# Masking the diagonal of attention on GpSimd, weighting later, and an early start for the last down projection

## The chip, the cores and the metric

One core of a Trainium2 chip. The metric is device time in microseconds (us), the median of several runs. The core's engines are TensorE (PE in the profile; its weight loads are PEld), VectorE (DVE), ScalarE (ACT), GpSimd (POOL) and SyncE (SP, which only starts transfers here).

## The reference, cut to what matters

Two transformer layers on x of shape (2, 512, 512), fp32 throughout, each with a modulation by c. Layer 0 has causal attention and a mixture of low-rank experts; layer 1 has a linear "attention" block, a gated feed-forward with low-rank additions, and a last gated feed-forward whose weights are 4-bit codes with scales.

```python
# layer 0, attention: 32 heads, 8 key/value groups of 4 heads, head width 16
scores = einsum('bihd,bjhd->bhij', q, k) * HD ** -0.5
scores = where(tril(ones((s, s))), scores, finfo.min)
out = einsum('bhij,bjhd->bihd', softmax(scores), v).reshape(b, s, -1) @ wo
...
# layer 1, twice (with low-rank terms the first time, without the second)
h = silu(x @ Wg.T) * (x @ Wu.T)        # 512 -> 1792
x = x + gb * (h @ Wd.T)                # 1792 -> 512
```

## The kernel before, in words

Every engine has one program written out by hand, and semaphores join them; there is no planner. TensorE's results are numbered jobs (`job_list`, line 114). Job j goes into PSUM bank j % 8, and `begin` (line 1373) waits until the job eight places earlier has been freed. Every fp32 product is made of three reduced-precision ones (lines 1383 to 1385): high by high, low by high, high by low, so each operand is rounded on ScalarE ("round") and its remainder subtracted on VectorE ("split").

*Attention* (lines 1472 to 1531 on TensorE). The work is 64 units: 2 batches by 8 groups by 4 query tiles of 128 rows. Unit n has ic = n % 4 and looks at ic + 1 key blocks, so units of a group are one, two, three and four blocks long. Step n of TensorE's loop has up to three parts:
- `scores(n)` (1477): for each of 4 heads a matmul (1485) and a bf16 matmul (1487) that adds -1e30 above the diagonal. Only the row maxima are taken from these. The two halves (heads 0, 1 and heads 2, 3) wait for the maxima of unit n-1, and VectorE's `reduce_max` (1178) makes two maxima per unit.
- `transposed(n - 2)` (1491): the scores again, key by query, one matmul per block (1500) with the maxima subtracted through extra rows of QS. GpSimd writes these rows (659) as the product of the identity and the maxima, two instructions per unit. For the diagonal block a bf16 matmul (1503) adds the mask. ScalarE takes the exponential of each block (798) into one of 10 tiles PT. Three PSUM banks (4 to 6) take the blocks in turn.
- `weighted` (1508): for two units at once, in even steps, for units n-4 and n-3. Values by exponentials, 32-row tiles (1517), into bank 7 for a whole group.

When a group is complete, its numerators and denominators leave bank 7: for even groups on ScalarE (`copy_even`, 504, called at unit 4 of eight), for odd ones on VectorE (`copy_odd`, 1096, at unit 2 of the next eight). VectorE then handles the pair: `swap_sums` at unit 3, `invert` in two halves at 4 and 5, `divide` at 6. ScalarE rounds the divided heads (`round_heads`, at the units in `ROUND_AT`, line 80) and VectorE splits them (`split_heads`, `SPLIT_AT`). Decoding of the 4-bit weights of layer 1 rides along: curves on ScalarE (758), their sums on VectorE (1066, at units 0, 1 and 7 of eight), scaling and adding in halves on GpSimd (615, 629).

After the loop VectorE splits the output weights WO (1199), which ScalarE rounds near the end (810), the remaining heads, the last pair's copy, swap, reciprocals and division (1200 to 1209), while TensorE multiplies the output projection `wo`; GpSimd subtracts weights (676) and adds the results to x (643).

*Layer 1, feed-forward, n = 0 and 1* (lines 1628 to 1699). `gu`: 14 pieces of gate and up, 48 or more matmuls each. For n = 0 a thin product `td` follows (1656). Then `gates` (1430), two small products that spread the gate row over the partitions, which VectorE copies into GAB (1038). Then `down`: eight banks for the eight row tiles; for n = 0 first x1 is added by identity matmuls (1666); then for each of 14 hidden tiles k and each row tile three matmuls (1680 to 1682). The hidden tile k is rounded into HH[k % 4] (912) and split into HL[k % 4] (1094). HH and HL also hold the input of gate up, so `round_hidden` of the first four waits for gate up's last matmul (906). At the end of `gu`, VectorE's order is: two hidden splits, weight piece split and scaling, for n = 1 then the gate copies (1343), then the rest. TensorE asks for all eight banks before the first matmul of `down` (1660).

## Time and profile before

| | us |
|---|---|
| median of 3 runs | 995.11 |
| lowest, highest | 993.63, 998.77 |
| the profiled execution | 996.45 |
| its span | 994.7 |
| TensorE busy, of the span | 913.2 (92%) |
| VectorE | 684.5 (69%) |
| ScalarE | 528.1 (53%) |
| GpSimd | 190.6 (19%) |
| the attention loop | about 88 to 292 |
| last gate up ends, last down starts | 900.1, 907.6 |

A matmul's busy time includes its way through the pipeline, so the distance between starts says more than its length. In a row of the timeline the columns are start, length, engine, line, operation, output and inputs, count, and in brackets the idle time before it with what ended it. In a row of groups the columns are line, engine, operation, names and shapes, count, busy us and mean ns of one, and the idle time before them with its releasers.

### The profile page before, as it was taken

Reading aid. Unit: us, or ns where it says so; the run is one execution under the profiler, and the core shown is the slowest. Engines: PE = TensorE matmul, PEld = TensorE weight load, DVE = VectorE, ACT = ScalarE, POOL = GpSimd, SP = SyncE. Lnnn points to the kernel's source line nnn. Section 1 sums busy time; section 2 is a strip of 40 time slices with the busy share of each in tenths; the row PEclk is TensorE's granted clock in tenths of the full one; section 3 lists DMA queues with packets and bytes.
Section 4 is the critical chain, followed back from the end, with each engine's and each line's share of the span. In section 5 each row is a group of like instructions: output and inputs, shape, how many; then the busy total and the mean of one; then the engine's idle time right before and its main releaser. Section 6 shows DMA issues by size and latency. Waiting matters only on the chain.

```text
span 994.7 us, 13863 instructions
## 1 busy us (share of the span) xinstructions
PE 913.2 (92%) x5316; PEld 702.4 (71%) x5316; DVE 684.5 (69%) x853; ACT 528.1 (53%) x683; POOL 190.6 (19%) x197
## 2 busy tenths in 40 slices
PE   3798899989899799999999999999969999997996
PEld 1565565555557587788888888688858888885885
DVE  4735788889989687777555554367887675666742
ACT  1503656666663335577555554267718666655730
POOL 3002546566666024100000000000040000000003
PEclk9798999999999899999999999789989999998999
DMA  9387466566422022016332332023302333332102
GB/s 330 125 240 148 60 109 105 67 107 107 81 86 96 11 64 74 22 40 192 96 95 87 95 88 71 1 85 106 106 22 77 95 104 106 86 105 64 43 1 84
DMA packets 40161, 91.60 MB, mean 92 GB/s; under 512 B 6944, under 2 KB 10144, under 8 KB 40096
## 3 DMA queue, kind: packets, MB, share of 16 engines
q1 hardware_dynamic: 35824, 85.23, 34.0%
q10 hardware_dynamic: 4272, 5.49, 1.6%
q8 instruction: 42, 0.69, 0.3%
q14 instruction: 23, 0.19, 0.1%
HBM read 76.02 MB, written 2.10 MB: 79 GB/s over the span
## 4 chain that ended last, share of the span: by engine, by line
PE 68%; DVE 6%; issue 3%; ACT 1%; POOL 1%; POOLq 0%; DVEq 0%; ACTq 0%
PE PS L1383 14%; PE PS L1385 14%; PE PS L1384 14%; PE PS L1680 5%; PE PS L1681 5%; PE PS L1682 5%; PE PS L1485 1%; PE PS L1517 1%; PE PS L1666 1%; PE PS L1616 1%; PE PS L1615 1%; POOL X L643 1%; DVE MX L1178 1%; PE PS L1500 1%; PE PS L1423 1%
## 5 line engine op out<-in xcount | busy, mean ns | idle before, releaser
L758 ACT ACTIVATE PL<-CODE 128x1024 f32<-128x1024 int32 x200 | 201.5, 1055 | 45.4 <-DVE ACC L1066 41.4
L1383 PE MATMUL PS<-HH,WRH 128*128 128x512 f32 x448 | 174.8, 390 | 0.0
L1384 PE MATMUL PS<-HH,WRL 128*128 128x512 f32 x448 | 174.5, 390 | 0.0
L1385 PE MATMUL PS<-HL,WRH 128*128 128x512 f32 x448 | 174.5, 390 | 0.0
L643 POOL TENSOR_TENSOR X<-X,SCR 128x512 f32<-128x512 f32 x32 | 42.2, 1328 | 601.4 <-DVE SCR L1051 601.3
L1066 DVE SCALAR_TENSOR_TENSOR ACC<-PL,ACC 128x1024 f32<-128x1024 f32 x100 | 124.5, 1245 | 8.4
L798 ACT ACTIVATE PT<-PS 128x512 f32<-128x512 f32 x160 | 85.2, 604 | 66.7 <-PE PS L1500 47.9
L1331 DVE TENSOR_TENSOR HID<-SG,PS 128x512 f32<-128x512 f32 x56 | 38.3, 685 | 114.2 <-PE PS L1616 68.4
L1178 DVE TENSOR_REDUCE MX<-PS 128x2 f32<-128x256 f32 (+3 forms) x128 | 99.5, 818 | 18.6 <-PE PS L1487 11.2
L659 POOL TENSOR_TENSOR QS<-ident,MX 64x256 fp32r<-64x256 f32 x128 | 97.1, 759 | 66.2 <-DVE MX L1178 59.2
L1485 PE MATMUL PS<-KS,QS 128*128 128x128 f32 (+3 forms) x256 | 84.0, 410 | 15.9 <-DVE MX L1178 14.4
L1383 PEld LDWEIGHTS PS<-HH,WRH 128*128 128x128 f32 x448 | 84.4, 188 | 17.6
L1384 PEld LDWEIGHTS PS<-HH,WRL 128*128 128x128 f32 x448 | 84.4, 188 | 17.6
L1385 PEld LDWEIGHTS PS<-HL,WRH 128*128 128x128 f32 x448 | 84.2, 188 | 17.4
L1680 PE MATMUL PS<-WRH,HH 128*128 128x512 f32 x224 | 89.3, 399 | 5.4 <-DVE GAB L1038 5.4
L1681 PE MATMUL PS<-WRL,HH 128*128 128x512 f32 x224 | 89.0, 397 | 0.0
L1682 PE MATMUL PS<-WRH,HL 128*128 128x512 f32 x224 | 88.8, 397 | 0.0
L1066 DVE SCALAR_TENSOR_TENSOR ACC<-PL 128x1024 f32<-128x1024 f32 x50 | 62.1, 1243 | 14.2 <-ACT PL L758 14.0
L930 ACT ACTIVATE SG<-PS 128x512 f32<-128x512 f32 x56 | 32.7, 589 | 73.3 <-PE PS L1616 46.1
L1485 PEld LDWEIGHTS PS<-KS,QS 128*128 128x128 f32 x256 | 51.1, 201 | 28.9 <-issue 13.8
L767 ACT ACTIVATE ACC<-ACC 128x1024 f32<-128x1024 f32 x50 | 53.1, 1062 | 31.1 <-DVE ACC L1066 31.1
L1500 PE MATMUL PS<-QS,KN 128*128 128x512 f32 x160 | 58.1, 443 | 7.4 <-ACT PT L798 7.0
(222 smaller groups left out, 1590.1 us busy)
## 6 DMA issues: line engine op xcount, KB each, us to landing
CODE<-in_CODES SPq DMA_DIRECT2D x50, 512.0 KB, 3.5
SCALE<-in_SCALES SPq DMA_DIRECT2D x100, 256.0 KB, 4.2
WM<-in_WM SPq DMA_DIRECT2D x12, 1024.0 KB, 7.2
QS<-FH SPq DMA_DIRECT2D x32, 128.0 KB, 4.1
QS<-FL SPq DMA_DIRECT2D x32, 128.0 KB, 5.2
X<-in_X ACTq DMA_DIRECT2D x2, 1024.0 KB, 12.4
out_x<-X ACTq DMA_DIRECT2D x8, 256.0 KB, 2.0
WF<-in_LBGU SPq DMA_DIRECT2D x14, 128.0 KB, 2.0
```

Source lines behind the costliest of these rows:

```text
L659: nc.gpsimd.tensor_tensor(QS[64:P, q % STACKS, :, ic * P + 64 * half:ic * P + 64 * half + 64], ident[rows, rows].unsqueeze(1).to_broadcast ...
L758: nc.scalar.activation(PL[:, n % 3], CODE[:, p % 2], ACT.Prelu, scale=scale, bias=bias, alpha=alpha).then_inc(s_plane, 1)
L798: nc.scalar.activation(block_of(n, jc)[:].rearrange("p h i -> p (h i)"), PS[:, 4 + done % 3], ACT.Exp, scale=HD ** -0.5).then_inc(s_exp, 1)
L1066: nc.vector.scalar_tensor_tensor(acc, PL[:, at_plane % 3], CAPS[i], rest_of, ALU.min, ALU.add).then_inc(s_used, 1)
L1178: nc.vector.reduce_max(MX[:, n % 2, 2 * pair:2 * pair + 2], PS[:, 2 * pair:2 * pair + 2, 0:w], AX_X).then_inc(s_mx, 1)
L1383: nc.tensor.matmul(dst, lh, rh, start=start and k == 0, stop=False)
L1384: nc.tensor.matmul(dst, ll, rh, start=False, stop=False)
L1385: ins = nc.tensor.matmul(dst, lh, rl, start=False, stop=stop and k == KC - 1)
L1485: nc.tensor.matmul(PS[:, h, 0:(ic + 1) * P], QS[:, q % STACKS, h, ic * P:(ic + 1) * P], KS[:, q % STACKS, 0:(ic + 1) * P], start=True, sto ...
L1680: nc.tensor.matmul(dst[t], hh, wh, start=(n == 1 and k == 0), stop=False, skip_group_check=True)
L1681: nc.tensor.matmul(dst[t], hh, wl, start=False, stop=False, skip_group_check=True)
L1682: ins = nc.tensor.matmul(dst[t], hl, wh, start=False, stop=last and n == 1, skip_group_check=True)
```

## The change

Four parts. (1) The bf16 mask matmul on the transposed diagonal block goes. GpSimd instead runs an `affine_select` over the diagonal block of exponentials in PT (128 x 512, zero where the key is behind the query), one per unit, before it waits for the maxima of the unit three later; TensorE's weighting waits for it. (2) Weighting moves from even steps (units n-4, n-3) to odd ones (n-5, n-4). `copy_even` and `copy_odd` come two units later, and so do swap and reciprocals; the division goes to unit 0 of the next eight. The last but one pair's division, rounding and split move behind the loop. (3) The gates of the last down projection are made after the last norm instead of after gate up. Its first hidden tile gets buffers of its own (HF, LF0), and is rounded and split after piece 7 of gate up. (4) Both down projections ask for each bank at its first use.

```diff
-ROUND_AT = {41: 0, 46: 1, 49: 2, 54: 3, 58: 4, 60: 5, 62: 6}
+ROUND_AT = {41: 0, 46: 1, 49: 2, 54: 3, 59: 4, 61: 5}
...
+            def cut(n):
+
+                block = block_of(n, n % TB)
+                pool.wait_ge(s_exp, STC(n // TB) + (n % TB + 1) * (n % TB + 2) // 2)
+                nc.gpsimd.affine_select(block[:], block[:], [[0, REP], [1, P]], ALU.is_ge, 0.0, base=0,
+                                        channel_multiplier=-1).then_inc(s_tri, 1)
+                pool.wait_ge(s_tri, n + 1)
+
             for n in range(B * GROUPS * TB):
                 q, ic = divmod(n, TB)
+                if n >= 3:
+                    cut(n - 3)
                 pool.wait_ge(s_mx, 2 * n + 2)
...
+            for n in range(B * GROUPS * TB - 3, B * GROUPS * TB):
+                cut(n)
             for half in range(2):
                 scale_half(N_QKV - 1, half)
...
-                if n % 8 == 4:
+                if n % 8 == 6:
                     copy_even(act, n // TB - 1)
...
+            round_heads(B - 1, PAIRS - 2)
             act.wait_ge(s_pv, units)
...
             def round_hidden(n, k):
-                i = HS_N[n] + k
-                if k < 4:
+                if (n, k) == (1, 0):
+                    act.wait_ge(s_mm, J["down", 0, NT - 1] + 1)
+                elif k < 4:
                     act.wait_ge(s_mm, J["gu", n, MC - 1, B - 1, 1] + 1)
...
+                    if (n, m) == (1, MC // 2):
+                        round_hidden(1, 0)
...
-                for k in range(2):
+                for k in range(n, 2):
                     round_hidden(n, k)
...
-                if pair_at(n, 2) is not None:
-                    copy_odd(pair_at(n, 2))
-                if pair_at(n, 3) is not None:
-                    swap_sums(pair_at(n, 3))
+                if pair_at(n, 4) is not None:
+                    copy_odd(pair_at(n, 4))
+                if pair_at(n, 5) is not None:
+                    swap_sums(pair_at(n, 5))
                 for half in range(2):
-                    if pair_at(n, 4 + half) is not None:
+                    if pair_at(n, 5 + half) is not None:
                         invert(half)
-                if pair_at(n, 6) is not None:
-                    divide(pair_at(n, 6))
+                if n >= 16 and n % 8 == 0:
+                    divide(n // 8 - 2)
...
-            for pair in range(PAIRS, last):
+            for pair in range(PAIRS, last - 1):
                 split_heads(pair)
+            divide(last - 1)
             copy_odd(last)
             gates("ga0")
             swap_sums(last)
+            split_heads(last - 1)
...
+                    if (n, m) == (1, MC // 2):
+                        hidden_split(1, 0)
...
-                if n == 1:
-                    gates(f"g{n}")
...
                 if n == 0:
                     modulate(3, B - 1)
+                    gates("g1")
...
-                                           QS[:, q % STACKS, :, ic * P:(ic + 1) * P], start=True, stop=jc < ic)
-                    if jc == ic:
-                        ins = nc.tensor.matmul(dst, maskB[:], identB[:].unsqueeze(1).to_broadcast([P, REP, P]),
-                                               start=False, stop=True)
+                                           QS[:, q % STACKS, :, ic * P:(ic + 1) * P], start=True, stop=True)
...
-                    pe.wait_ge(s_exp, blocks[1])
+                    if jc < ic:
+                        pe.wait_ge(s_exp, blocks[1])
+                    else:
+                        pe.wait_ge(s_tri, n + 1)
...
-            for n in range(units + 3):
+            for n in range(units + 4):
...
-                if n >= 3 and n % 2 == 0:
-                    for unit in (n - 4, n - 3):
+                if n >= 5 and n % 2 == 1:
+                    for unit in (n - 5, n - 4):
                         weighted(unit)
...
-                gates(f"g{n}", 1, n)
-                dst = [begin(("down", n, t)) for t in range(NT)]
+                if n == 0:
+                    gates("g0", 1, 0)
+                dst = [PS[:, bank(("down", n, t))] for t in range(NT)]
...
+                        if (n, k) == (1, 0):
+                            begin(("down", n, t))
...
                 if n == 0:
                     for b in range(B):
                         norm(3, b)
+                    gates("g1", 1, 1)
```

In the order of jobs the two gates of n = 1 move likewise, behind the last norm.

## Rows read from the trace of the kernel before

**Rows 1.** Table by stage: stretch, its length, PE, PEld, DVE, ACT, POOL busy, PEclk, DMA share, GB/s.

```profile
92.00:292.00 200.00, 179.79 (x2002) 116.62 (x2002) 170.22 (x201) 125.16 (x212) 116.03 (x143) 0.99 0.55 89
...
800.00:900.00 100.00, 100.00 (x443) 82.67 (x441) 62.79 (x61) 61.19 (x71) 0.00 (x0) 1.00 0.32 95
...
908.00:912.00 4.00, 4.00 (x11) 3.03 (x11) 3.90 (x4) 2.15 (x3) 0.00 (x0) 0.50 0.36 87
```

**Rows 2.** Groups on VectorE from 92 to 292 us; the last one over the whole run.

```profile
L1178 DVE TENSOR_REDUCE MX<-PS 128x2 f32<-128x1024 f32 x32 | 37.7, 1219 | 8.1 <-issue 4.4 <-PE PS L1487 3.1 <-DVE NUM L1119 0.4
L1178 DVE TENSOR_REDUCE MX<-PS 128x2 f32<-128x768 f32 x32 | 29.2, 953 | 6.0 <-PE PS L1487 4.1 <-POOL QS L659 1.5
L1114 DVE RECIPROCAL DENS<-DENS 128x256 f32<-128x256 f32 x14 | 24.4, 1743 | 0.0
L1178 DVE TENSOR_REDUCE MX<-PS 128x2 f32<-128x512 f32 x30 | 19.3, 683 | 3.3 <-PE PS L1487 3.0
L1066 DVE SCALAR_TENSOR_TENSOR ACC<-PL,ACC 128x1024 f32<-128x1024 f32 x12 | 16.3, 1358 | 0.0
L1178 DVE TENSOR_REDUCE MX<-PS 128x2 f32<-128x256 f32 x30 | 11.4, 417 | 0.5 <-PE PS L1487 0.3
...
L1102 DVE SCALAR_TENSOR_TENSOR NUM<-PS,HALVES,NUM 128x512 f32<-128x512 f32 x7 | 5.3, 751 | 7.0 <-PE PS L1517 7.0
...
L1119 DVE TENSOR_TENSOR NUM<-NUM,DENS 128x512 f32<-128x512 f32 x7 | 4.8, 681 | 0.0
...
L1066 DVE SCALAR_TENSOR_TENSOR ACC<-PL,ACC 128x1024 f32<-128x1024 f32 x100 | 124.5, 1245 | 8.4
```

**Rows 3.** Timeline of TensorE in attention, from 200.13 to 225.33 us.

```profile
200.13 0.38 PE L1485 MATMUL PS<-KS,QS 128*128 128x256 f32 x1
...
203.01 0.52 PE L1485 MATMUL PS<-KS,QS 128*128 128x384 f32 x1
...
204.32 0.48 PE L1500 MATMUL PS<-QS,KN 128*128 128x512 f32 x1
204.64 0.39 PE L1503 MATMUL PS<-identB,maskB 128*128 128x512 bf16 x1
204.96 1.74 PE L1517 MATMUL PS<-PT,V 128*32 128x128 f32 x56
206.62 0.50 PE L1485 MATMUL PS<-KS,QS 128*128 128x512 f32 x1
...
208.08 0.71 PE L1500 MATMUL PS<-QS,KN 128*128 128x512 f32 x2
...
225.33 0.38 PE L1485 MATMUL PS<-KS,QS 128*128 128x256 f32 x1
```

**Rows 4.** The chain of waits from 240 to 270 us, shares of the 30 us.

```profile
by line: DVE MX L1178 19.9%; issue 16.5%; PE PS L1485 12.0%; DVE DENS L1114 11.1%; PE PS L1517 11.1%; ACT PT L798 7.3%; PE PS L1500 4.6%; PE PS L1487 3.5%; ACT PL L758 3.1%; PE PS L1503 3.1%; DVE DENS L1110 2.5%; DVE NUM L1119 2.0%; DVE DEN
```

**Rows 5.** Timeline of TensorE at the start of the last down projection.

```profile
900.18 1.98 PE L1435 MATMUL PS<-MR,sel 2*128 2x512 f32 x4
907.56 0.76 PE L1680 MATMUL PS<-WRH,HH 128*128 128x512 f32 x1 [5.40 <-DVE GAB L1038]
```

**Rows 6.** Groups on GpSimd: the diagonal products from 92 to 292 us, the others over the run.

```profile
L659 POOL TENSOR_TENSOR QS<-ident,MX 64x256 fp32r<-64x256 f32 x126 | 95.1, 754 | 63.4 <-DVE MX L1178 56.5
...
L643 POOL TENSOR_TENSOR X<-X,SCR 128x512 f32<-128x512 f32 x32 | 42.2, 1328 | 601.4 <-DVE SCR L1051 601.3
...
L607 POOL MEMSET KN<- 64x512 f32 x2 | 1.0, 520 | 44.9 <-PE PS L1452 44.8
```

**Rows 7.** The even copies on ScalarE, from 92 to 292 us.

```profile
L509 ACT ACTIVATE NUM<-PS,HALVES 128x512 f32<-128x512 f32 x8 | 5.5, 688 | 8.3 <-PE PS L1517 8.3
```

**Rows 8.** Timeline behind the attention loop: the last division on VectorE, a subtraction on GpSimd.

```profile
297.74 4.61 POOL L676 TENSOR_TENSOR ATL<-ATF,ATH 128x2048 fp32r<-128x2048 f32 x1
...
300.82 2.08 DVE L1119 TENSOR_TENSOR NUM<-NUM,DENS 128x512 f32<-128x512 f32 x1
```

**Rows 9.** Timeline of TensorE at the start of the first down projection.

```profile
634.93 0.30 PE L1666 MATMUL PS<-identR,HH 128*128 128x128 f32 x1 [0.88 <-DVE GAB L1038]
```

More of the change, by code:

```diff
@@ L179, in job_list @@
                 jobs.append((("td", b), 1))
-        gates(f"g{n}")
+        if n == 0:
+            gates("g0")
         for t in range(NT):
@@ L319, in build @@
         LDBL = sb("LDBL", [P, D], F32R, R0 + 96 * K)
+        HF = sb("HF", [P, T], F32R, R0 + 86 * K)
+        LF0 = sb("LF0", [P, T], F32R, R0 + 94 * K)
         SCR = sb("SCR", [P, 2, D], F32, R0 + 100 * K)
@@ L363, in build @@
         s_exp = sem("exponentials_ready")
+        s_tri = sem("diagonal_blocks_cut")
         s_pv = sem("values_weighted")
@@ L525, in hidden_used, with hidden_parts @@
                 eng.wait_ge(s_mm, J["down", n, NT - 1] + 1)
+        def hidden_parts(n, k):
+            return (HF[:], LF0[:]) if (n, k) == (1, 0) else (HH[:, k % 4], HL[:, k % 4])
         def tile_transposed(eng, u):
@@ L1093, in hidden_split @@
                 dve.wait_ge(s_hsh, HS_N[n] + k + 1)
-                nc.vector.tensor_tensor(HL[:, k % 4], HID[:, k], HH[:, k % 4], ALU.subtract).then_inc(s_hsl, 1)
+                high, low = hidden_parts(n, k)
+                nc.vector.tensor_tensor(low, HID[:, k], high, ALU.subtract).then_inc(s_hsl, 1)
             def copy_odd(pair):
@@ L1338, in _ @@
                         rest(TDL[:, cols], ("td", b), TDH[:, cols])
-                    gates(f"g{n}")
-                for k in range(2):
+                    gates("g0")
+                for k in range(n, 2):
                     hidden_split(n, k)
                 finish(p)
-                if n == 1:
-                    gates(f"g{n}")
                 for i in range(MC // 2):
@@ L1368, in _ @@
                     modulate(3, B - 1)
+                    gates("g1")
         @block.tensor
@@ L1676, in _ @@
                         cols = slice(t * P, (t + 1) * P)
-                        hh, hl = HH[:, k % 4, cols], HL[:, k % 4, cols]
+                        high, low = hidden_parts(n, k)
+                        hh, hl = high[:, cols], low[:, cols]
+                        if (n, k) == (1, 0):
+                            begin(("down", n, t))
                         wh, wl = WRH[:, slot(p), w], WRL[:, slot(p), w]
```

4 lines of the change are left out of this document (3 added, 1 removed).

## The prediction

> **What bounds the kernel now.** I read the page first (its chain of work that ended last is TensorE for 68% of the span), then a table by stage, then the two stages that the diff touches. Two kinds of stage appear. In the projections TensorE never stops, and only its own gaps are worth anything. In attention (92 to 292 us) no engine fills the time: of 200 us VectorE is busy 170.2, GpSimd 116.0, ScalarE 125.2 [rows 1]; TensorE's 179.8 overlaps its own pipeline and says less. That stage is a relay. Scores of unit n+1 wait, half by half, for the row maxima of unit n, and VectorE's next maxima wait for those scores, so roughly each unit costs the longer of what TensorE and what VectorE do in it.
>
> VectorE's share of a unit is two maxima, 0.84, 1.36, 1.9 or 2.44 us for the four lengths, plus whatever rides on that unit: reciprocals of 1.74, curve sums of 1.36, a division of 0.68, copies of 1.5 for numerator and denominator with a wait of 1.0 before them [rows 2]. TensorE's share is read from one stretch of its timeline [rows 3]: scores take 1.3 us for the third unit of a group (203.01 to 204.32) and 1.46 for the fourth, a transposed block 0.28 to 0.32, weighting two long units 1.66 (204.96 to 206.62). The chain passes through both engines [rows 4].
>
> The second place is the start of the last down projection. Gate up ends at 900.1, four gate matmuls start, and then TensorE idles 5.40 us for the gate copies, which VectorE makes only after two hidden splits and two weight pieces; its next full matmul is at 907.56 and TensorE's granted clock is 0.50, its 1.2 GHz level, from 908 to 912 [rows 1, 5].
>
> **The change part by part.**
>
> *Mask on the scores goes from TensorE.* 64 bf16 matmuls leave. The next instruction starts 0.32 us behind one (204.64 to 204.96) [rows 3]; 64 of them are at most 20 us of TensorE's time, and nothing where TensorE waits anyway. The row maxima keep their own mask matmuls. Only what is on the chain counts: in the 30 us of [rows 4] L1503 has 3.1%, 0.93 us, four masks of about nine.
>
> *Mask goes to GpSimd.* 64 selections over 128x512 in fp32, each waiting for the exponential and then for itself. None is in the trace. Below it lies a fill of 64x512, no input, 0.52 us; above, a 128x512 operation of two inputs, 1.33 us [rows 6]. One input lies between; the middle is 0.92, rounded to 0.90, which I take, keeping both ends. GpSimd then has 116.0 + 64 x 0.90 = 174 us, and with about 0.07 us between dependent instructions (some 210 of them; two diagonal products of 0.61 come as 1.30 in the timeline) 189 us. That fits under 200, with little spare. Behind the selection on its queue stand the diagonal products of unit n, which TensorE needs two steps later, and VectorE's next but one maxima; a unit of slack hides the selection as long as GpSimd's sum stays under the stage. The row of diagonal products shows that slack: GpSimd sat idle 56.5 us there for maxima [rows 6].
>
> The Trainium skill (GPSIMD Engine Reference, section 3.1) gives 1.8 cycles an element at best for a one-input style loop, 769 ns for 512 elements; by that figure GpSimd would stand at 180 us instead of 189 and the sum would not change. No row here shows it.
>
> *Weighting one step later, copies and divisions two units later.* Waits leave: VectorE stood 7.0 us before seven odd copies, ScalarE 8.3 us before eight even ones, because the weighting was issued in the same step as the copy [rows 2, 7]. Now it is a step old when the copy asks. But the load is dealt out anew. TensorE's step n is scores (0.6, 1.0, 1.3, 1.46 by the length), the transposed blocks of unit n-2 (3, 4, 1, 2 of 0.3), a mask of 0.25, and in every second step a weighting (1.66 for a long pair, 24/56 of it, 0.7, for a short one). Eight units, step by step:
> - before, TensorE 2.5, 2.5, 3.5, 2.3 twice; VectorE 2.2, 2.7, 3.4, 3.2, 2.6, 3.1, 2.6, 3.8. The larger of each pair, summed: 24.9. The trace has 25.2, from 200.13 to 225.33 [rows 3].
> - after, TensorE 1.5, 2.9, 1.6, 3.7 twice (weighting now shares a step with the long fourth unit); VectorE 2.9, 2.7, 1.9, 2.4, 2.3, 3.8, 3.6, 3.8, since swap, reciprocals and division stand at the sixth unit, the seventh and the next first. The larger of each pair: 25.0.
>
> So pair by pair nothing is won: TensorE's relief falls where VectorE was already the longer. What is won comes from slack between neighbours. VectorE's own sum is 22.5 in eight units (13.1 of maxima, 2.25 curve sums, 6.4 for the pair of groups) and cannot shrink; its idle time is 2.7. Afterwards I find one real hole, at the fourth unit (TensorE 3.7 + 0.6 for the next scores, VectorE 2.4: 1.5 us when it has no arrears and the hand-offs are taken in), and small ones of 0.4 together. Idle 1.9 instead of 2.7, eight times: **-6 us**. The bounds are VectorE's sum (-21) and no gain at all (0).
>
> Against that stands contention. A division that takes 0.68 us elsewhere took 2.08 for the last pair, and ended at 302.90, half a microsecond after GpSimd's 4.61 us subtraction that ran from 297.74 [rows 8]. Some 30 VectorE instructions of two inputs in memory lie in the stage; curve sums average 1.36 us there [rows 2] against 1.25 for one that nothing disturbs (the mean of all 100 of the run, most of them with GpSimd idle), a loss of 0.11 with GpSimd 58% busy. At some 95% busy that is 0.18: 30 x 0.07 = **+2 us**. If each of the 30 lost half a selection, as that division lost more, it would be 30 x 0.45 = +13, and the kernel would end at 995 us. The Trainium skill (SBUF - State Buffer, "Who interferes with whom") has such an exclusion, for the whole instruction, of a VectorE instruction with two SBUF inputs and a GpSimd instruction that reads SBUF. By that rule the trace agrees in kind; its average of 0.11 is smaller.
>
> *End of attention.* The weighting of units 60 and 61 (0.8 us) moves behind the last transposed block; the even copy (1.4) now stands before the rounding of the output weights in place of a head's rounding (0.65), and VectorE already waits 3.6 us for that rounding; one division (0.7) moves into VectorE's tail. The last selection is covered by 2.3 us of weighting. Masks saved, 0.5. **+1 us** (0 to 3).
>
> *First down projection.* Its banks are asked for one by one, so the additions of x1 start when the gate matmuls are through, and not after the copies, for which TensorE idled 0.88 us before 634.93 [rows 9]: **-1 us**.
>
> *Second down projection.* The gates are made before gate up, and the first hidden tile is rounded and split into its own buffers in the middle of it (about 1.0 us of ScalarE and 1.2 of VectorE; both are busy some 62 of 100 us in gate up while TensorE is busy all of them [rows 1], so free). At its end TensorE goes straight on: the first tile's 24 matmuls last 5.4 us, in which the second is rounded (1.0) and split (1.2), and the last bank is wanted after 4.8 us. From 900.1 to 907.56 are 7.5 us; 11 matmuls at the 1.2 GHz level [rows 1], starting 0.43 us apart against 0.226 in gate up (443 in 100 us), cost 0.2 us too much each, 2.2. What returns is the gates' four matmuls, 1.7 us, now in front of gate up where TensorE is the bound. 7.5 + 2.2 - 1.7 = **-8 us**. If the clock falls anyway it is -6.
>
> **Sum.** -6 + 2 + 1 - 1 - 8 = -12. The profiled execution took 996.45 us (span 994.7), 1.3 above the median of 995.11; 996.45 - 12 = 984.45. I say **984 us**; by the median it would be 983.
>
> **The rivals.**
> 1. *Attention gains nothing.* The larger of each pair decides, or two-input instructions lose to GpSimd what the holes give: 0 in the stage, 0 + 1 - 1 - 8, so 988 us (995 with the full 13 on top of -6). For it: the pair sum above and the division of 2.08. Against: VectorE visibly catches up between units. 0.17, and 0.03 for the 995.
> 2. *GpSimd becomes the pace, and the kernel slower.* Its stage is 116.0 + 15 of hand-offs + 64c. From c = 1.08 us it passes 200; from about 1.2 it eats the other gains. At the two-input price of 1.33 (with the blocking that the row holds, [rows 6]) it is 216, +16 in place of -4: 16 + 1 - 1 - 8 = +8, so 1004 us. For it: the price is unknown and the engine's spare time small; TensorE would then wait for diagonal products. Against: one input, not two. 0.14 for slower, and 0.12 for a price of 1.1 to 1.25, where the time stays within 5 us of before.
> 3. *The last down projection doesn't start early:* ScalarE's rounding of the second tile, queued behind the last gate up, comes late. 1.0 + 1.2 us against 5.4 say no; then only the other terms stay, -4, so 992 us. 0.04.
>
> **How the numbers follow.** Forecast 0.5; rivals 0.2, 0.26 in two parts, 0.04. Range 971 to 1001: below, the attention bound of -21 with no contention gives 967, of which I take all but the last 4 us; above, rival 2 nearly to its price. Faster by over 0.5% (5 us, about what can be told from no change): 0.5 + 0.17 + 0.01 of rival 3 = 0.68; within: 0.12 + 0.03 + 0.03 = 0.18; slower: 0.14.
>
> **What would show it.** L1503 gone; 64 selections of 0.6 to 1.1 us, GpSimd busy near 175 us in the stage; copies with no wait for weighting; the stage 3 to 5 us shorter; VectorE busy still 170; waits of TensorE for diagonal products near 0. In the last down projection no idle before its first matmul and full clock through it. Wrong if the selections take over 1.1 us, or if waits for QS by L659 appear on TensorE or VectorE.

## The result: 1012.84 us, slower

Changed kernel: 1012.84 us, median of 4 runs (1011.61 to 1014.15). The kernel before beside it: 996.94 us (993.63 to 1003.13). Ratio 1.0152, 95% interval 1.0098 to 1.0207. I had said 984 us, 971 to 1001. The profiled execution took 1011.61 us, its span is 1009.9 (before 994.7), so the trace has 15.2 us to explain.

Three marks split the span: the start of the last pair of row maxima on VectorE (A), the start of the first transpose of LQF, the weight tile that TensorE turns behind the output projection (B), and the end. A is read from these rows, before and after:

```profile
282.64 2.36 DVE L1178 TENSOR_REDUCE MX<-PS 128x2 f32<-128x1024 f32 x2 [0.44 <-DVE NUM L1119]
```
```profile
303.49 2.36 DVE L1204 TENSOR_REDUCE MX<-PS 128x2 f32<-128x1024 f32 x2
```

| | A | A to B | B to end |
|---|---|---|---|
| before | 282.6 | 34.2 | 677.9 |
| after | 303.5 | 39.3 | 667.1 |
| difference | +20.9 | +5.1 | -10.8 |

So the stretch with the down projections is shorter by about what was forecast, and attention took back more than twice that. The profile after, first the page's busy times and TensorE's granted clock in tenths by fortieths of the span:

```profile
PE 912.9 (90%) x5252; PEld 704.8 (70%) x5252; DVE 691.2 (68%) x853; ACT 527.4 (52%) x683; POOL 229.5 (23%) x261
...
PEclk9798799998999989999999999979997999999999
```

The table by stage (columns as in [rows 1]):

```profile
92.00:292.00 200.00, 163.97 (x1683) 108.31 (x1686) 157.52 (x184) 109.91 (x187) 140.73 (x188) 0.92 0.53 82
800.00:900.00 100.00, 100.00 (x443) 82.84 (x443) 68.28 (x67) 64.82 (x75) 0.00 (x0) 1.00 0.33 97
```

VectorE, my bound of the stage, is busy 157.5 of 200 us instead of 170.2: it waits more. And the clock is new: 0.92 where [rows 1] has 0.99. The groups that answer to [rows 2, 6, 7], from VectorE (92 to 292), GpSimd (whole run) and ScalarE (92 to 292):

```profile
L1204 DVE TENSOR_REDUCE MX<-PS 128x2 f32<-128x768 f32 x30 | 27.8, 954 | 15.8 <-PE PS L1516 15.7
...
L1204 DVE TENSOR_REDUCE MX<-PS 128x2 f32<-128x512 f32 x30 | 19.4, 686 | 8.8 <-POOL QS L678 6.6 <-PE PS L1516 1.9
L1091 DVE SCALAR_TENSOR_TENSOR ACC<-PL,ACC 128x1024 f32<-128x1024 f32 x12 | 16.3, 1362 | 0.0
...
L1145 DVE TENSOR_TENSOR NUM<-NUM,DENS 128x512 f32<-128x512 f32 x6 | 6.7, 1117 | 0.0
...
L1128 DVE SCALAR_TENSOR_TENSOR NUM<-PS,HALVES,NUM 128x512 f32<-128x512 f32 x6 | 4.5, 742 | 0.0
```
```profile
L678 POOL TENSOR_TENSOR QS<-ident,MX 64x256 fp32r<-64x256 f32 x128 | 88.0, 687 | 41.4 <-DVE MX L1204 33.0
L666 POOL TENSOR_SCALAR_AFFINE_SELECT PT<-PT 128x512 f32<-128x512 f32 x64 | 48.0, 750 | 8.6 <-ACT PT L819 4.0
```
```profile
L514 ACT ACTIVATE NUM<-PS,HALVES 128x512 f32<-128x512 f32 x7 | 4.9, 702 | 0.0
```

The selection costs 0.75 us (0.90 forecast), and the copies' waits for weighting are gone as forecast (0.0 where 7.0 and 8.3 stood). What took their place is in the waits from 88 to 312 us (the engine and line that waits, what it waits for, then us in all, how often, and the longest):

```profile
ACT PT L819 <- PE PS L1529: 96.3, 52, 3.6
...
PE PS L1529 <- ACT PT L819: 18.1, 14, 3.0
...
DVE MX L1204 <- POOL QS L678: 13.6, 9, 2.2
...
PE PS L1529 <- POOL QS L678: 10.4, 9, 1.6
```

Before, the last two kinds were 1.5 us [rows 2] and 0.3, and TensorE's wait for ScalarE's exponentials was 7.0. So TensorE waits for ScalarE to empty a PSUM bank, and TensorE and VectorE wait for GpSimd's diagonal products. TensorE's wait for ScalarE comes about once per eight units, here unit 8k+6 with the even copy, a curve pair, then the four exponentials of unit 8k+7:

```profile
222.29 1.58 ACT L819 ACTIVATE PT<-PS 128x512 f32<-128x512 f32 x3 [2.63 <-PE PS L1529]
...
223.74 0.70 ACT L514 ACTIVATE NUM<-PS,HALVES 128x512 f32<-128x512 f32 x1
...
224.31 0.71 ACT L514 ACTIVATE DEN<-PS,HALVES 128x512 f32<-128x512 f32 x1
...
224.88 2.03 ACT L779 ACTIVATE PL<-CODE 128x1024 f32<-128x1024 int32 x2
...
226.77 2.08 ACT L819 ACTIVATE PT<-PS 128x512 f32<-128x512 f32 x4
...
227.44 0.50 PE L1529 MATMUL PS<-QS,KN 128*128 128x512 f32 x1 [2.71 <-ACT PT L819]
```

TensorE stands 2.71 us. Before, its longest gap between 100 and 280 us was 1.03 us and its clock 1.00 throughout; now it has twelve gaps over 1.1 us there, and over the 20 us from 220 the clock is 0.91.

### The profile page after: what moved, and what is told of

Read it like the earlier page. It is cut to its first block, busy times and chain, and to the rows that moved or that the text cites. A ratio compares the mean times of both kernels' runs of the same rounds, so it can differ in the third digit from the quotient of the medians.

```text
span 1009.9 us, 13854 instructions
## 1 busy us (share of the span) xinstructions
PE 912.9 (90%) x5252; PEld 704.8 (70%) x5252; DVE 691.2 (68%) x853; ACT 527.4 (52%) x683; POOL 229.5 (23%) x261
## 4 chain that ended last, share of the span: by engine, by line
PE 73%; DVE 10%; POOL 5%; issue 5%; ACT 4%; DMA 1%; POOLq 0%; SPq 0%; DVEq 0%; ACTq 0%
PE PS L1412 15%; PE PS L1413 14%; PE PS L1414 14%; PE PS L1715 5%; PE PS L1716 5%; PE PS L1717 5%; PE PS L1514 3%; DVE MX L1204 3%; POOL QS L678 2%; ACT PT L819 2%; PE PS L1546 2%; PE PS L1529 1%; DVE DENS L1140 1%; DMA WM<-in_WM 1%; PE PS L1645 1%
## 5 line engine op out<-in xcount | busy, mean ns | idle before, releaser
L1204 DVE TENSOR_REDUCE MX<-PS 128x2 f32<-128x256 f32 (+3 forms) x128 | 100.4, 820 | 39.3 <-PE PS L1516 24.9
L1514 PE MATMUL PS<-KS,QS 128*128 128x128 f32 (+3 forms) x256 | 89.2, 427 | 14.3 <-DVE MX L1204 12.0
L678 POOL TENSOR_TENSOR QS<-ident,MX 64x256 fp32r<-64x256 f32 x128 | 88.0, 687 | 41.4 <-DVE MX L1204 33.0
L1529 PE MATMUL PS<-QS,KN 128*128 128x512 f32 x160 | 60.6, 462 | 28.8 <-ACT PT L819 18.1
L1715 PE MATMUL PS<-WRH,HH 128*128 128x512 f32 x216 | 85.0, 393 | 0.0
L1716 PE MATMUL PS<-WRL,HH 128*128 128x512 f32 x216 | 84.9, 393 | 0.0
L1717 PE MATMUL PS<-WRH,HL 128*128 128x512 f32 x216 | 84.7, 392 | 0.0
L1514 PEld LDWEIGHTS PS<-KS,QS 128*128 128x128 f32 x256 | 55.2, 218 | 31.0 <-DVE MX L1204 18.7
```

What stands on the lines that cost most here:

```text
L678: nc.gpsimd.tensor_tensor(QS[64:P, q % STACKS, :, ic * P + 64 * half:ic * P + 64 * half + 64], ident[rows, rows].unsqueeze(1).to_broadcast ...
L1204: nc.vector.reduce_max(MX[:, n % 2, 2 * pair:2 * pair + 2], PS[:, 2 * pair:2 * pair + 2, 0:w], AX_X).then_inc(s_mx, 1)
L1514: nc.tensor.matmul(PS[:, h, 0:(ic + 1) * P], QS[:, q % STACKS, h, ic * P:(ic + 1) * P], KS[:, q % STACKS, 0:(ic + 1) * P], start=True, sto ...
L1715: nc.tensor.matmul(dst[t], hh, wh, start=(n == 1 and k == 0), stop=False, skip_group_check=True)
L1716: nc.tensor.matmul(dst[t], hh, wl, start=False, stop=False, skip_group_check=True)
L1717: ins = nc.tensor.matmul(dst[t], hl, wh, start=False, stop=last and n == 1, skip_group_check=True)
```

## The experiments

Theories at the start. **Q**: the selections stand ahead of the diagonal products on GpSimd's queue and wait there for ScalarE. **L**: GpSimd's sum of work. **S**: the new schedule costs by itself, because the even copy and curves now stand before the exponentials of the long fourth unit. Later texts call S in its narrower forms C (ScalarE's burst of copy and curves leaves TensorE without a free bank), "clock" (the gaps then lower TensorE's clock) and W (the later weighting itself is what costs), and L "pace". All results, with marks A and B and the clock over 92 to 292 us from each profiled execution:

| kernel | median, us | ratio, 95% | clock | A | A to B | B to end |
|---|---|---|---|---|---|---|
| e1 down alone | 989.3 | 0.987 to 0.995 | 0.99 | 282.9 | 34.1 | 667.2 |
| e2 mask on TensorE | 1011.8 | 1.009 to 1.019 | 0.92 | 299.9 | 38.0 | 674.7 |
| e3 selection alone | 1030.2 | 1.030 to 1.036 | 0.89 | 317.5 | 33.0 | 678.1 |
| e4 cut behind | 1022.3 | 1.020 to 1.030 | 0.91 | 310.3 | 37.7 | 672.1 |
| e5 curves behind | 1002.7 | 0.999 to 1.007 | 0.96 | 295.8 | 37.3 | 670.1 |
| e6 e2, gap filled | 1000.5 | 1.000 to 1.005 | 0.99 | 290.2 | 34.1 | 673.5 |
| e7 weighting even | 1027.3 | 1.025 to 1.034 | 0.88 | 322.7 | 33.5 | 669.0 |
| e8 e5 with cut | 1013.1 | 1.011 to 1.022 | 0.89 | 306.3 | 37.7 | 673.5 |
| e9 after, filled | 1010.0 | 1.009 to 1.016 | 0.96 | 297.0 | 40.4 | 670.5 |
| e10 curves ahead | 1002.2 | 1.000 to 1.008 | 0.96 | 290.4 | 38.0 | 674.7 |
| e11 e9, scale later | 996.6 | 0.997 to 1.002 | 0.96 | 289.1 | 40.2 | 670.4 |
| e12 e11, ATL later | 993.1 | 0.990 to 0.998 | 0.99 | 284.9 | 34.2 | 672.1 |
| e13 mended | 992.2 | 0.992 to 0.996 | 0.95 | 285.2 | 36.3 | 668.7 |
| e14 burst planted | 1014.8 | 1.011 to 1.019 | 0.95 | 299.3 | 36.7 | 668.8 |
| e15 e13, filled | 992.0 | 0.990 to 0.996 | 0.96 | 284.4 | 34.2 | 672.1 |
| e16 e14, filled | 1002.9 | 1.004 to 1.008 | 0.97 | 298.1 | 34.7 | 671.2 |

The medians of the kernel before in these sessions were 996.1 to 999.0.

**The change taken apart: e1 to e3.** e1 is the kernel before with the edits of the two down projections only. e2 is the changed kernel with the mask matmul put back and no selection. e3 is the kernel before with the selection only:

```diff
 # e2, from the changed kernel
-                if n >= 3:
-                    cut(n - 3)
...
-                                           QS[:, q % STACKS, :, ic * P:(ic + 1) * P], start=True, stop=True)
+                                           QS[:, q % STACKS, :, ic * P:(ic + 1) * P], start=True, stop=jc < ic)
+                    if jc == ic:
+                        ins = nc.tensor.matmul(dst, maskB[:], identB[:].unsqueeze(1).to_broadcast([P, REP, P]),
+                                               start=False, stop=True)
...
-                    if jc < ic:
-                        pe.wait_ge(s_exp, blocks[1])
-                    else:
-                        pe.wait_ge(s_tri, n + 1)
+                    pe.wait_ge(s_exp, blocks[1])
```

> Only the two down projections are changed (parts 3 and 4): early gates, own buffers for the first hidden tile, banks asked for one by one. All theories of the attention stage expect the same: the attention loop as before (last row maximum near 285 us) and about 9 us less in all, a ratio near 0.991. If instead the time is as before, the gain of the last down projection is given back somewhere behind it.

> The changed kernel with the selections taken out and the mask matmul back on TensorE; weighting, copies and divisions stay late. Theory Q (GpSimd's queue: the selection stands before the diagonal products and waits for ScalarE) and theory L (GpSimd's sum of work) expect the attention stage at or under its time of before, the kernel at 985 to 990 us. Theory S (the new schedule itself costs: even copy and curves stand before the exponentials of the long fourth unit) expects the stage to stay some 15 us longer, the kernel near 1010 us.

> The kernel before with the selection alone (mask matmul off TensorE, selection on GpSimd before the maxima wait); weighting in even steps, copies and down projections as before. Theory S expects it at or under the time before, 985 to 997 us. Theories Q and L expect it slower by 10 us or more, 1005 to 1025 us, since TensorE now even has one step less between exponential and weighting.

e1 gives 8 us and is the fastest of the three kernels so far. e2 is as slow as the whole change: without one selection the schedule alone moves A from 282.9 to 299.9. That is theory S; Q and L, which expected 985 to 990 us, do not explain the bulk of the loss. For e3 it is the other way round: S expected 985 to 997 us, Q and L a loss, and the selection costs 33 us, since the weighting in even steps asks for its result at once. The waits of e3, 88 to 312 us:

```profile
PEld PS L1530 <- POOL PT L658: 32.7, 19, 2.9
PE PS L1530 <- POOL PT L658: 29.1, 20, 2.4
```

TensorE waits there for the selected block itself, which neither Q nor L had. The later weighting is thus what makes room for the selection; together they come out near where the schedule alone does (3.6 us behind it at A).

**Where the selection stands: e4** puts `cut(n - 3)` behind the diagonal products of unit n.

```diff
-                if n >= 3:
-                    cut(n - 3)
                 pool.wait_ge(s_mx, 2 * n + 2)
...
                     pool.wait_ge(s_dg, 2 * n + half + 1)
+                if n >= 3:
+                    cut(n - 3)
```

> The changed kernel with each selection moved behind the two diagonal products of its step on GpSimd's queue instead of before them. The work on every engine is the same. Theory Q expects most of the loss back, 985 to 995 us, and waits for QS near 0. Theory L expects no more than 3 us of difference from the changed kernel (1010 us), theory S none.

Worse by 9.5 us: the weighting now waits for the selection (PE L1546 on PT L666, below). Q was half right: the waits for QS fell as it said, from 10.4 to 1.2 us on TensorE and from 13.6 to 1.0 on VectorE, but the time that it expected back did not come, since the selection is late for the weighting instead. L and S, which expected little or no difference, didn't have that wait either.

```profile
PEld PS L1546 <- POOL PT L666: 17.1, 14, 2.0
...
PE PS L1546 <- POOL PT L666: 13.4, 13, 1.8
```

**What in the schedule costs: e5, e6, e7, e10**, all on e2. e5 runs the curves of unit 8k+6 behind unit 8k+7, e10 ahead of the copy, behind 8k+5. e6 leaves everything in place and issues one product of TensorE seven times, in front of the gap (each time afresh, so the result is the same). e7 puts the weighting back into even steps.

```diff
 # e5
                     copy_even(act, n // TB - 1)
-                ride(n + 3)
+                else:
+                    if n % 8 == 7:
+                        ride(n + 2)
+                    ride(n + 3)
 # e10
                     copy_even(act, n // TB - 1)
-                ride(n + 3)
+                else:
+                    ride(n + 3)
+                if n % 8 == 5:
+                    ride(n + 4)
 # e6
-                    ins = nc.tensor.matmul(dst, KN[q % STACKS][:, jc * P:(jc + 1) * P],
+                    for x in range(7 if n % 8 == 7 and jc == 2 else 1):
+                        ins = nc.tensor.matmul(dst, KN[q % STACKS][:, jc * P:(jc + 1) * P],
```

> The kernel with the new schedule and the mask still on TensorE (e2_mask_on_tensore, 1011.8 us), with one edit: on ScalarE the curves that followed the even groups' copy (behind unit 8k+6) run behind the exponentials of unit 8k+7. Theory C (ScalarE's burst of copy and curves ahead of the long fourth unit leaves TensorE without a free bank, and the gap then halves TensorE's clock for some microseconds): the gaps of 1.3 to 2.9 us ahead of the fourth unit's last transposed block shrink below 1 us, the granted clock over 92 to 292 us goes from 0.92 back above 0.96, and the time comes to 995 to 1002 us. Theory W (weighting two units at a time at odd steps, one unit later, is itself what costs): 1008 to 1014 us, clock unchanged.

> e2_mask_on_tensore with the gap filled and nothing moved: in every unit 8k+7 the third transposed block's product is issued seven times instead of once (each time afresh, the last one counts), which is work for about 1.3 to 1.5 us in the place where TensorE otherwise waits for ScalarE. Theory C with the clock as the larger part: the granted clock over 92 to 292 us rises above 0.96 although six useless products per eight units are added, and the time falls to 998 to 1006 us. If the wait itself is the cost and the clock only goes with it: 1010 to 1014 us or, where the products are not hidden, up to 1020 us.

> e2_mask_on_tensore with the weighting put back to the even steps; copies, swaps and divisions stay two units later. Theory W: 988 to 995 us, since the later weighting is the costly part. Theory C: ScalarE's copy and curves still stand ahead of the fourth unit, so the gaps and the clock of 0.92 stay and the time is 1006 to 1014 us.

> e2_mask_on_tensore with the curves that followed the even groups' copy moved ahead of it, behind unit 8k+5 (e5 moved them behind unit 8k+7, which made VectorE wait up to 4.2 us for their planes and so left gaps before the scores). Theory clock: neither gap is left, clock over 92 to 292 us 0.98 or more, 992 to 999 us. If the later weighting costs by itself even without gaps, as e6's 1000.5 us with useless products allows: 999 to 1004 us with the clock at 0.98 or more.

e6 is the telling one: 48 useless products on the busiest engine make the kernel 11 us faster, and A comes 9.7 us earlier. Nothing else was moved. The stage in e2, then in e6:

```profile
92.00:292.00 200.00, 177.24 (x1802) 113.82 (x1802) 159.29 (x189) 111.94 (x190) 105.58 (x134) 0.92 0.54 83
```
```profile
92.00:292.00 200.00, 186.35 (x1954) 122.60 (x1955) 167.66 (x198) 116.56 (x200) 110.98 (x140) 0.99 0.53 82
```

Only A speaks for the clock of the stage. Another 3.9 us of the gain in these two profiled executions lie between A and B: there a split on VectorE took 4.67 us in e2, since it started behind a long GpSimd subtraction, and 0.87 in e6, where it started before it, and the clock was 0.91 in e2 and 1.00 in e6. TensorE's wait is hardly longer in sum in e2 than in e1: its two groups with idle time, of e1 and then of e2, 92 to 292 us, hold 21.8 and 23.8 us of it.

```profile
L1498 PE MATMUL PS<-KS,QS 128*128 128x384 f32 (+3 forms) x248 | 81.9, 412 | 14.5 <-DVE MX L1190 14.5
L1513 PE MATMUL PS<-QS,KN 128*128 128x512 f32 x160 | 58.1, 443 | 7.3 <-ACT PT L806 7.0 <-POOL QS L667 0.3
```
```profile
L1510 PE MATMUL PS<-KS,QS 128*128 128x384 f32 (+3 forms) x239 | 85.4, 437 | 6.5 <-DVE MX L1200 6.2
...
L1525 PE MATMUL PS<-QS,KN 128*128 128x512 f32 x146 | 54.6, 455 | 17.3 <-ACT PT L815 15.9 <-POOL QS L676 1.1
```

It had become lumpy. TensorE's timeline in e2, behind one such gap:

```profile
224.90 0.80 PE L1525 MATMUL PS<-QS,KN 128*128 128x512 f32 x1 [2.71 <-ACT PT L815]
...
228.09 0.67 PE L1510 MATMUL PS<-KS,QS 128*128 128x384 f32 x1
...
228.66 0.67 PE L1510 MATMUL PS<-KS,QS 128*128 128x384 f32 x1
...
231.79 0.47 PE L1510 MATMUL PS<-KS,QS 128*128 128x512 f32 x1
...
232.14 0.47 PE L1510 MATMUL PS<-KS,QS 128*128 128x512 f32 x1
```

At 228 a score matmul of 384 columns with its mask comes every 0.57 us; at 231.8 one of 512 columns, a longer one, every 0.35. From 224.7 to 231.5 the granted clock is 0.50, TensorE's 1.2 GHz level. Between 100 and 290 us it is so four times, for 23.8 us together, each time behind a gap of 1.8 to 2.9 us. The Trainium skill (TensorE: Matmul & The Clock Gate, "HAM oscillation — how this bites in real kernels") describes matmul groups that each start at half rate because TensorE idled ahead of them; the trace agrees in kind. e5 and e10 made that gap shorter without useless work and gained 9 us each, somewhat less than expected: e5 made VectorE wait up to 4.2 us for the planes (what the curves leave for its sums), e10 keeps gaps of 1.1 to 1.7 us and a clock of 0.96, not the 0.98 of its forecast. In e7 the weighting of the next group asks for bank 7 before the late copy has emptied it; late copies need the late weighting:

```profile
PEld PS L1542 <- ACT DEN L514: 17.1, 7, 2.5
...
PE PS L1542 <- ACT DEN L514: 14.5, 7, 2.2
```

So C's forecast for e7 missed by 13 us, and e7 doesn't test W, since it brings a wait of its own. What speaks against W as the main cause is that e5, e6 and e10 leave the late weighting where it is and gain 9 to 11 us. That it costs a part isn't excluded: e6, at a clock of 0.99, is still 7.3 us behind e1 at A, and no run separates late weighting, burst and useless products in that.

**What GpSimd adds: e8, e9, e11, e12.** e8 is e5's edit, e9 e6's, on the changed kernel. e11 is e9 with the scaling and adding of decoded weights one unit later. e12 is e11 with ATL's subtraction behind the residual additions.

```diff
 # e11
-                    scale_at[n + 1 + half] = p, half
+                    scale_at[n + 2 + half] = p, half
                     if p >= 2:
-                        add_at[(n + 3 if p < 4 else B * GROUPS * TB - 3) + half] = p, half
+                        add_at[(n + 4 if p < 4 else B * GROUPS * TB - 3) + half] = p, half
 # e12
-            split_weight(ATL, ATF, ATH, 2)
...
             for t in range(TB, NT):
                 add_gated(("wo", t))
+            split_weight(ATL, ATF, ATH, 2)
```

> The changed kernel (selection on GpSimd) with the same edit as e5_curves_behind_fourth. Theory C: ScalarE's gaps go, but those that TensorE has behind GpSimd's diagonal products (1.1 to 1.6 us, nine of them) stay, so the gain is about half of that of e5: 1002 to 1008 us with a clock near 0.94. If the selection is a gain once the schedule is mended, it is at or under e5's time. Theory W: 1008 to 1014 us.

> The changed kernel itself with the same filling as e6_gap_filled (third transposed block of every unit 8k+7 issued seven times), which took 11 us off the kernel without the selection. Theory clock (short gaps of TensorE halve its clock, and that is the larger part of the loss): ScalarE's gaps close, GpSimd's gaps of 1.1 to 1.6 us behind the diagonal products stay, so the clock over 92 to 292 us rises from 0.92 to about 0.95 and the time comes to 1003 to 1008 us. Theory pace (with the selection GpSimd sets the pace, so filling TensorE gives nothing): 1010 to 1015 us with the last row maximum still starting near 311 us.

> e9_gap_filled_cut with GpSimd's scaling and adding of the decoded weights one unit later, so that GpSimd no longer waits for ScalarE's fold with diagonal products queued behind it. Theory clock: some of the gaps behind the diagonal products go, the clock over 92 to 292 us rises by 0.01 to 0.03 over e9's, and the time is 3 to 8 us under e9's. Theory pace (GpSimd's sum of work, not its wait for the fold, makes the diagonal products late): the same as e9 within 2 us.

> e11_filled_scale_later (996.6 us) with GpSimd's subtraction for ATL moved behind the last residual addition of the attention's output product. In e11 the third last head split took 4.19 us beside that 4.60 us subtraction, and from the last row maxima to the LQF transposes 40.2 us passed, where e1 and e6 show 34.1. If the overlap of the two subtractions is what made the end of attention longer: the split is back at 0.7 to 0.9 us, the stretch at 34 to 36 us, and the time falls by 4 to 6 us, to 991 to 993 us. If something else queues there (the selections themselves): unchanged at 996 to 998 us. If ATL then comes late for the next products: 998 us or more.

e8 gained nothing (1002 to 1008 was expected). Its waits for QS were halved (4.8 us on TensorE), but e5's side effect came with the edit: VectorE waits 12.8 us for planes, up to 4.5 at a time, and TensorE then has gaps of up to 2.6 us before the scores. e9 gained only 3 us (6.5 at A): gaps behind the diagonal products stay. In e11 they go. TensorE's waits for QS in e9, then in e11, 88 to 312 us:

```profile
PE PS L1530 <- POOL QS L678: 10.9, 11, 1.6
```
```profile
PE PS L1530 <- POOL QS L678: 1.8, 2, 1.6
```

e11 is 13 us under e9 in the medians, more than the 3 to 8 expected, and 8.1 us in the profiled executions, with a clock of 0.96 in both: by these two traces the gain is in the waits. So GpSimd's sum of work (theory L, "pace"), which is the same in both, was not what made the products late; it was one blocked instruction. The first `scale_half` of a piece waits for the fold, ScalarE's last step on it, for 2.0 to 6.3 us in the changed kernel and 2.1 to 5.3 in e9, starts 0.13 us behind it, and selections and products queue behind it. In e11 no such wait is left. e12 is for the end of attention. In the changed kernel, VectorE and GpSimd, from 319.41 us (ATL is the remainder of a weight for the next products):

```profile
319.41 4.61 POOL L697 TENSOR_TENSOR ATL<-ATF,ATH 128x2048 fp32r<-128x2048 f32 x1
...
320.39 4.17 DVE L1152 TENSOR_TENSOR FL<-NUM,FH 128x512 fp32r<-128x512 f32 x1
```

and the same split in e12:

```profile
301.84 0.69 DVE L1152 TENSOR_TENSOR FL<-NUM,FH 128x512 fp32r<-128x512 f32 x1
```

A split of 0.69 us took 4.17 and ended half a microsecond behind the subtraction. Apart, A to B is back at 34.2 from e11's 40.2. Not all of that is the split: from A to B the clock was 0.92 in e11 and 1.00 in e12. e13 has the same order at the end at a clock of 0.91 there, and takes 36.3 us, so by these traces some 4 of the 6 us are the overlap and some 2 the clock. In the medians e12 is 3.4 us under e11, in the ratios to the kernel before (0.9995 and 0.9936) 6 us. For this instruction the trace agrees with the rule that the prediction quotes from the Trainium skill (SBUF - State Buffer, "Who interferes with whom"): the split reads two SBUF operands, and it ended only when the subtraction was over.

**The repairs together, and a counter-test: e13 to e16.** e13 is the changed kernel with the edits of e10, e11 and e12 and no useless product; e15 adds four products per eight units. e14 is e1 (old schedule, no selection) with ScalarE's last exponential of unit 8k+6 made three times more; e16 is e14 with e6's filling.

```diff
 # e14
+                    for x in range(3 if n % 8 == 6 and jc == ic else 0):
+                        nc.scalar.activation(block_of(n, jc)[:].rearrange("p h i -> p (h i)"), PS[:, 4 + done % 3],
+                                             ACT.Exp, scale=HD ** -0.5).then_inc(s_again, 1)
+                        act.wait_ge(s_again, 3 * (n // 8) + x + 1)
```

> The changed kernel with the three repairs and no useless product: curves ahead of the even copy (as e10), GpSimd's scaling and adding one unit later (as e11), ATL's subtraction behind the residual additions (as e12). Theory clock: the gaps of TensorE over 1 us are mostly gone, the clock over 92 to 292 us is 0.97 or more, and the time is 985 to 993 us, with the selection worth up to 4 us over e1 (989.3 us) at best. If gaps of 1 us and a little more remain and are enough for the clock to fall (as in e10, 0.96): 993 to 1000 us.

> e1_down_alone (989.3 us: old attention schedule, no selection) with a planted burst: ScalarE repeats the last exponential of every unit 8k+6 three times more (about 1.9 us per eight units, 15 us in all, on an engine that is idle for 83 of the 200 us of attention). Theory clock: the fourth unit's blocks come late, TensorE shows gaps over 1 us there, its clock falls below 0.96 over 92 to 292 us, and the time rises by 8 to 20 us, to 997 to 1009 us. If the loss belonged to the new schedule only (late weighting, late copies) and not to such a burst: 989 to 992 us.

> e13_mended (992.2 us, clock 0.95 over 92 to 292 us, seven TensorE gaps of 1.06 to 2.2 us behind ScalarE) with the third transposed block of every unit 8k+7 issued five times instead of once. Theory clock: the gaps of the fourth unit shrink under 1 us, the clock over 92 to 292 us rises to 0.98 or more, and the time is 983 to 989 us, at or under e1_down_alone (989.3). If the later end of attention in the new order (copies, divisions and cuts left for the end) takes it back: 990 to 994 us.

> e14_burst_planted (1014.8 us; e1 with 1.9 us more work on ScalarE per eight units) with TensorE's gap filled as in e6 (third transposed block of every unit 8k+7 issued seven times). ScalarE's burst stays whole, only TensorE's idle time is turned into useless work. Theory clock: clock over 92 to 292 us back to 0.98 or more, and most of the 25 us come back: 992 to 1000 us. If the burst costs by the wait itself: 1010 to 1020 us.

e14 has a loss of this size without any part of the new attention schedule: 25 us for about 15 us of work on an engine that had 75 of 200 us free (ScalarE 124.87 busy in e1). Its stage, with e1's above it:

```profile
92.00:292.00 200.00, 179.76 (x2001) 116.68 (x2001) 170.12 (x202) 124.87 (x212) 115.62 (x143) 0.99 0.55 89
```
```profile
92.00:292.00 200.00, 173.48 (x1821) 111.27 (x1821) 159.14 (x192) 124.78 (x212) 105.16 (x134) 0.95 0.54 83
```

e16 took back 12 of the 25 us in the medians, not the most of it that I expected. Here the profiles help little: e14's profiled execution (1006.6 us) was its fastest, e16's (1005.9) its slowest, and A is nearly the same in both (299.3, 298.1). The wait itself, ScalarE's burst in full length, is therefore a large part of e14's loss. How large can be estimated from the mean clock that is on record for every execution, not only for the profiled ones. With the same instructions e5 ran from 994.7 us at 0.973 to 1009.0 at 0.955, e11 from 990.7 at 0.973 to 1001.7 at 0.959, e15 from 983.2 at 0.976 to 993.8 at 0.964: 8 to 9 us for each 0.01 of an execution's mean clock. Between the medians of e14 (0.956) and e16 (0.971) that makes 12 us, all that the filling took back; between e1 (0.967) and e14 it makes 9 of the 25 us. The clock doesn't account for every spread: the kernel before took 994.0 us at 0.969 and 1003.6 at 0.967.

e13 and e15 are faster than the kernel before, and not to be told apart from e1 (0.987 to 0.995 against 0.992 to 0.996 and 0.990 to 0.996). Their clock of 0.95 and 0.96 is under the 0.97 and 0.98 that I expected. In e15 it stands at 0.50 from 103.9 to 110.7, behind a wait of 2.13 us for row maxima that e9 and e11 have there too and that the filling doesn't touch, and from 202.9 to 206.2, where TensorE has no gap over 1 us; why it fell there is open. e15's useless products brought nothing in the median; three of its nine executions, those with a mean clock of 0.967 or more, took 983.2 to 987.5 us, the others 992.0 to 993.8. So with every repair the change to attention as a whole, selection and schedule, is worth nothing that can be measured over e1. What the selection alone is worth on a mended schedule no run shows: e10, which has the mask on TensorE, lacks the repair at the end of attention.

## Why the prediction was wrong

*Attention, -6 and +2: the step that failed.* The step is the pair sum, in which each unit costs the longer of TensorE's and VectorE's work, with one hole of 1.5 us at the fourth unit. A moved by +20.9 us where -4 was forecast. The pair sum left ScalarE out. I moved `copy_even` from the light unit 8k+4 to 8k+6 and never asked what stands behind it on ScalarE's queue: a curve or two, then the four exponentials of the longest unit, whose PSUM bank TensorE wants next. "TensorE 3.7 against VectorE 2.4" counted as a hole at the fourth unit; in the trace it is where TensorE waits up to 3.02 us. The second half of the step is the clock, which I had read in [rows 1] for the down projection and took for granted in attention. Its share there: e2 and e6 differ by the filling alone, 0.92 to 0.99 and 9.7 us at A; e11 and e12 have the same instructions up to A, 0.96 and 0.99 and 4.2 us. Both give 1.4 us for each 0.01, so the 0.07 that the change lost is some 10 of its 20.9 us, and waits are the other half. This division is an estimate from two pairs. The mean clocks of whole executions agree with it: the medians are 0.967 for e1 and 0.952 for the changed kernel, which at 8 to 9 us for each 0.01 makes 12 to 14 of the 23.5 us between these two, the end of attention included.

The -6 had a slip in it, too. VectorE's sum in eight units is given as 22.5, but the parts named (13.1, 2.25 and 6.4) make 21.75, and [rows 1] (170.22 of 200) give 21.4 in 25.2 us, so its idle time before was 3.8 and not 2.7. The right sum would have made the forecast gain larger, so it is not what turned the sign.

*Selection at 0.90 us:* measured 0.75 in the mean and 0.63 where nothing disturbs it, inside my ends. GpSimd's busy time in the whole run rose by 38.9 us (190.6 to 229.5), 48 for the selections less faster diagonal products (687 against 754 ns). The sentence "a unit of slack hides the selection as long as GpSimd's sum stays under the stage" failed: the sum did stay under (140.7 of the 200 us), and QS was late all the same, behind the wait for the fold. The sign that I had named as one of being wrong, waits for QS, appeared. At A this is the smaller part: e2, without any selection, has 17.0 of e1's distance of 20.6 us to the changed kernel. Rival 2 had the right effect (slower) and the wrong reason; its price of 1.2 us or more was not met.

*Contention +2:* the divisions took 1117 instead of 681 ns, 2.6 us for six; curve sums hardly changed (1362, before 1358). Right in sum by luck: the curve sums did not lose the 0.07 us each that was forecast, the six divisions lost 0.44 each. It was not on the path that mattered.

*End of attention +1:* measured +5.1. I used [rows 8] for the division and did not ask which two-input instruction would stand beside the same 4.61 us subtraction in the new order. It was the split, 3.5 us longer (4.17 against 0.69); the division, freed of it, took 0.69 instead of 2.08. The new order does this without the selection, too: e2 has 38.0 us from A to B. The clock from A to B was 0.91, before 0.95.

*First down projection -1:* from the start of the gate matmuls to that of the first identity product were 2.86 us (632.07 to 634.93, [rows 9]), now 1.91 (657.99 to 659.90). Right.

*Second down projection -8:* its first matmul starts 0.23 us behind gate up's last, and the clock from 925 to 929 is 1.00.

```profile
925.16 0.39 PE L1715 MATMUL PS<-WRH,HF 128*128 128x512 f32 x1
```

Both down terms together are -10.8 against -9 in one pair of profiled executions, and e1's median is 8 us under the kernel before. Right, within a spread of several microseconds (last section).

*Copies' waits gone:* right, 0.0 us, and no gain came of it: 15 us of waits on engines whose own path was not the long one there.

## What to carry to other kernels

When work moves to another place in a relay of engines, write down what stands behind it on every queue that it is put on, also that of an engine that is busy only 60% of the time, and above all ahead of the longest unit. Watch TensorE's largest gaps and not only their sum: here nearly the same idle time (23.8 against 21.8 us) in gaps of 1.3 to 2.9 us instead of, with one exception, at most 1.0 went with a clock of 0.92 instead of 0.99 and cost some 10 us through it. To find out whether the clock is a cause, repeat a product in front of the gap: if useless work raises the granted clock and makes the stage itself end earlier, the clock had a share. Compare the medians and the clocks of all executions, too: in e14 and e16 the profiled ones alone would have hidden it.

## What was unexpected of the hardware

TensorE's clock fell to its 1.2 GHz level for 3 to 7 us behind single gaps, in a stage where TensorE was idle for only 24 of 200 us. It does not fall each time. Between 100 and 280 us e2 has seven gaps over 1.1 us; it fell behind those of 1.77, 2.28, 2.71 and 2.86 us and not behind those of 1.34, 1.61 and 1.92. In the changed kernel it fell behind six of twelve, the shortest of them 1.3 us, and in e14 and e15 once with no gap over 1 us in the 20 us ahead. Nor is it the same each time: e11 and e12 had gaps of 2.13 and 2.15 us at 103.23 and 102.46 us in the same instructions, and over 100 to 140 us clocks of 0.87 and 1.00:

```profile
100.00:140.00 40.00, 34.91 (x344) 23.20 (x347) 27.55 (x35) 21.63 (x38) 25.94 (x38) 0.87 0.47 58
```
```profile
100.00:140.00 40.00, 33.93 (x381) 22.92 (x379) 30.86 (x39) 23.97 (x41) 27.43 (x40) 1.00 0.49 61
```

The same shows behind attention. From B to the end the kernels with both down edits (the changed one, e1, e2, e4 to e16) have the same instructions but for where ATL's subtraction stands, yet take 667.1 to 674.7 us; over 700 to 800 us the clock was 0.95 in e1 and 0.91 in e2. A difference of under 8 us between two profiled executions there may be nothing else, which is why medians and the mark A were used above.
